# Routing each token to its own expert in the last stage of a two-layer attention kernel

## What is computed

```
x = x + _L1_xattn_ref(ctx, _layernorm(x), ...)      # ends with out @ Wout and a layer norm
x = x + _L1_ffn_ref(_layernorm(x), ...)

logits = xt @ Wg.T                                  # xt: 4096 x 512
top1 = argmax(logits)                               # one expert per token
xhat = layernorm(xt)
for each expert e:
    h = gelu((xhat * s_e + b_e) @ W1_e + b1_e)      # 512 -> 128
    y += (top1 == e) * (h @ W2_e + b2_e)            # 128 -> 512
```

## Time and profile before

| | |
|---|---|
| median of 3 runs | 3383.18 us (3382.89 to 3386.95) |
| profiled execution, its own time | 3382.07 us |
| its span, first to last instruction | 3380.3 us |
| TensorE matmuls busy | 3005.5 us, 89% |
| DVE, ACT, POOL busy | 2083.6, 1558.0, 1327.4 us |
| mean granted TensorE clock | 0.934 of 2.4 GHz |
| DMA | 220.43 MB, mean 65 GB/s |

### The profile page before, as it was taken

How to read it: one execution, slowest core, us unless ns; L and a number is a source line. 1 busy time by engine, 2 the same in 40 slices (tenths; PEclk the granted TensorE clock), 3 DMA queues, 4 the chain that set the end, 5 groups by cost and what they waited for, 6 DMA issues and landing times. The chain is left out here.

```text
span 3380.3 us, 44846 instructions
## 1 busy us (share of the span) xinstructions
PE 3005.5 (89%) x16620; PEld 2534.8 (75%) x16620; DVE 2083.6 (62%) x4123; ACT 1558.0 (46%) x3036; POOL 1327.4 (39%) x913
## 2 busy tenths in 40 slices
PE   6888999968664999999999999999999769999998
PEld 5677777744433898989899898989989657777777
DVE  4766666622365776767777676777767654444432
ACT  2333333311033676767667676766767522222222
POOL 1444444410021465656556565655656530111110
PEclk9899999977765999999999999999999979999999
DMA  5112121112078112121211112111121231111100
GB/s 178 36 46 60 48 61 39 48 66 95 3 267 318 46 34 61 36 61 37 62 37 34 59 37 62 37 59 35 36 62 37 79 127 35 68 50 50 50 25 25
DMA packets 131551, 220.43 MB, mean 65 GB/s; under 512 B 44750, under 2 KB 46799, under 8 KB 127246
## 3 DMA queue, kind: packets, MB, share of 16 engines
q1 hardware_dynamic: 117933, 168.09, 16.4%
q10 hardware_dynamic: 13408, 49.56, 4.0%
HBM read 112.01 MB, written 69.47 MB: 54 GB/s over the span
## 5 line engine op out<-in xcount | busy, mean ns | idle before, releaser
L1635 POOL TENSOR_SCALAR pa_Pr<-pa_Pr,pa_rs 128x590 f32<-128x590 f32 x512 | 904.6, 1771 | 699.9 <-DVE pa_rs L1864 699.9
L1868 DVE TENSOR_REDUCE pa_least<-pa_S 128x1 f32<-128x590 f32 x512 | 391.3, 764 | 242.3 <-PE pa_S L1699 240.4
L1764 ACT ACTIVATE pa_PTh<-pa_W 128x512 fp32r<-128x512 f32 (+1 forms) x640 | 367.7, 596 | 174.4 <-PE pa_W L1710 158.5
L1819 DVE TENSOR_TENSOR pa_PTl<-pa_W,pa_PTh 128x512 fp32r<-128x512 f32 (+1 forms) x640 | 422.0, 683 | 33.2 <-ACT pa_PTh L1764 25.4
L1796 ACT ACTIVATE pa_Pr<-pa_S,pa_least 128x590 f32<-128x590 f32 x512 | 385.2, 752 | 79.3 <-DVE pa_least L1868 76.2
L1710 PE MATMUL pa_W<-pa_ident,pa_Pr 128*128 128x128 f32 (+1 forms) x2560 | 368.7, 275 | 9.7 <-DVE pa_Ql L1834 8.9
L1710 PEld LDWEIGHTS pa_W<-pa_ident,pa_Pr 128*128 128x128 f32 (+1 forms) x2560 | 306.8, 143 | 34.0 <-DVE pa_Ql L1834 12.0
L1724 PE MATMUL pa_O<-pa_PTh,pa_V 128*128 128x512 f32 (+1 forms) x640 | 293.2, 458 | 11.6 <-DVE pa_PTl L1819 8.1
L1697 PE MATMUL pa_S<-pa_U,pa_Qh 128*128 128x296 f32 (+1 forms) x1024 | 234.1, 311 | 44.7 <-DMA pa_Um<-pa_U 44.4
L1725 PE MATMUL pa_O<-pa_PTl,pa_V 128*128 128x512 f32 (+1 forms) x640 | 257.8, 403 | 0.0
L1697 PEld LDWEIGHTS pa_S<-pa_U,pa_Qh 128*128 128x128 f32 x1024 | 180.3, 195 | 71.1 <-DMA pa_Um<-pa_U 47.7
(11 more groups left out here) (400 smaller groups left out, 7223.2 us busy)
## 6 DMA issues: line engine op xcount, KB each, us to landing
pa_Um<-pa_U SPq DMA_DIRECT2D x128, 147.5 KB
pa_Qh<-pa_Qh SPq DMA_DIRECT2D x128, 128.0 KB
o_s<-pa_O_pair SPq DMA_DIRECT2D x64, 256.0 KB, 2.6
ex_o_raw<-o_s SPq DMA_DIRECT2D x8, 2048.0 KB, 10.8
z_s<-la_z_hi ACTq DMA_DIRECT2D x8, 1180.0 KB, 7.6
z_s<-la_z_lo ACTq DMA_DIRECT2D x8, 1180.0 KB, 10.0
pa_z_hi<-z_s ACTq DMA_DIRECT2D x8, 1180.0 KB, 6.0
pa_z_lo<-z_s ACTq DMA_DIRECT2D x8, 1180.0 KB, 10.1
```

The source lines that it names most:

```text
L1635: pool.tensor_scalar(p, p, rs[:, g % 2, t:t + 1], None, ALU.mult).then_inc(*pool_s.mark("probs", n))
L1764: act.activation(out, src, ACT.Copy, scale=scale).then_inc(*act_s.mark("hi", *name))
L1819: dve.tensor_tensor(out, src, f32(hi_ap), ALU.subtract).then_inc(*dve_s.mark(*name))
L1868: dve.tensor_reduce(least[:, g % 2, t:t + 1], scored[n % 2], AX, ALU.min).then_inc(*dve_s.mark("least", n))
```

## The change

Layout. A scratch tensor `xs_s` in DRAM holds 4 regions of 4128 rows of 1028 floats: two experts share a region, one fills it from below and one from above. A row is a token's `xh`, its x, and its number (less 65536) in one column. `wt_s` holds for each expert 128 rows of 2561 floats: W1 high and low, W2 high and low, one column of b1 and a row part of b2.

First half, a round b for each batch (and one more to drain). It does what was done before up to `choice`, one batch behind `read_out`. `ranks` counts for each token how many earlier ones chose the same expert, by a matmul with a triangle of ones and one with running counts kept by POOL. `row_places` makes row numbers of this. POOL's `send(b)` writes the 512 rows of a batch to `xs_s` by four indirect DMAs. W1 and W2 pass through in 8 chunks, one per round, are split and stored to `wt_s`. x, xh and the number share three buffers R, and o has 12 slots in place of 8.

Between the halves, `routes()` computes on DVE from the counts of all experts which 15 tiles of 512 rows there are (15 are enough for any routing), each tile's expert, its rows and its end. Rows past the end and their output are out of bounds and skipped by the DMA.

Second half, 15 tiles i. POOL fetches the 512 rows of a tile (128 partitions by 4 rows) and the 128 rows of its expert's weights by index, and writes out 4 x 128 rows by token number. Weights have two buffers, rows have four.

```diff
+            def send(b):
+                pool.wait_ge(*dve_s.after("place", b))
+                pool.wait_ge(*dve_s.after("xh", b, NT - 1))
+                pool.wait_ge(*pool_s.after("token", b))
                 for t in range(NT):
+                    pool.indirect_dma_start(xs_s, bass.IndirectOffsetOnAxis(ap=place[:, b, t:t + 1], axis=0), R4[b % 3][:, t, :], None)\
+                        .then_inc(free[b % 3], 16)
...
+            def fetch_weights(i):
+                if i >= 2:
+                    pool.wait_ge(*pe_s.after("y", i - 2, NT - 1))
+                n = i % 2
+                pool.indirect_dma_start(f32(Wt[n][:, :]), None, wt_s, bass.IndirectOffsetOnAxis(ap=wsrc[:, i:i + 1], axis=0)).then_inc(wt_in[n], 16)
...
+            for i in range(TILES):
+                pool.wait_ge(*dve_s.after("tok", i))
+                for j in range(NT):
+                    pool.wait_ge(*dve_s.after("free", "y", i, j))
+                    pool.indirect_dma_start(out_rows, bass.IndirectOffsetOnAxis(ap=tok[:, i, j:j + 1], axis=0), R4[buf(i)][:, j, D:2 * D], None,
+                                            bounds_check=TOKENS - 1, oob_is_err=False).then_inc(free[buf(i)], 16)
+                if tile(i + 2):
+                    fetch_weights(i + 2)
+                if tile(i + 3):
+                    fetch_rows(i + 3)
...
+            for b in range(B + 1):
+                if batch(b):
+                    read_out(b, 0)
+                if batch(b - 1):
+                    transposed(b - 1)
+                if batch(b):
+                    read_out(b, 1)
+                if batch(b - 1):
+                    gate_logits(b - 1)
+                if batch(b):
+                    shifts(b)
+                    read_out(b, 2)
+                if batch(b - 1):
+                    gate_rows(b - 1)
+                if batch(b):
+                    read_out(b, 3)
+                if batch(b - 1):
+                    ranks(b - 1)
...
+            for i in range(TILES + 1):
+                first_product(i)
+                for j in range(NT):
+                    second_product(i - 1, j)
+                    row_columns(i + 1, j)
```

In the perceiver, SP fills `xs_s` with zeros, one piece per pair of heads behind `store`:

```diff
+            BLANKS = -(-blanks.shape[0] // PAIRS // 32) * 32
...
+                sp.dma_start(blanks[n0:n1, :].rearrange("(p k) t -> p k t", k=k),
+                             f32(Ql[0][0][P - part:P, :]).unsqueeze(1).to_broadcast([part, k, T])).then_inc(blank, 16)
```

In the slots stage, `S0T` and `WhhT` (in three pieces) are loaded first, and the `gh` products come ahead of the wait for `si`; the copies of `siT` on DVE move behind those of `gh`:

```diff
+            pe.wait_ge(S0_in, 16)
+            for n in range(3):
+                ps = unit("gh", n)
+                pe.wait_ge(Whh_in[n], 16)
...
+            pe.wait_ge(si_in, 16)
             for c in range(C):
                 ps = unit("siT", c)
```

More of the change, by code:

```diff
@@ L1174, in _ @@
                        .then_inc(*dve_s.mark("gh", n, c))
+            for c in range(C):
+                copy(("siT", c), siT[:, c, :])
             dve.wait_ge(*dve_s.at(0, "gh", 2, C - 1))
@@ L1943, in build_experts @@
[L1943 to L1949, removed]
+        Wt = [sb(f"Wt{n}", [P, WW], F32R) for n in range(2)]
@@ L2107, in shut @@
-            def shut(b, e):
-                pe.wait_ge(*dve_s.after("free", "hotT", b))
-                pe.matmul(bank_of["h", b, e][:, :], sel[:, e:e + 1].to_broadcast([P, HE]), hotT[:, :], start=False, stop=True).then_inc(*pe_s.mark("h", b, e))
-            def biases(b):
-                pe.wait_ge(small_cut, 2)
-                pe.wait_ge(*dve_s.after("free", "hotT", b))
-                for t in range(NT):
-                    ps = claim(pe, "out", b, t)
-                    pe.matmul(ps[:, :], hotT[:, t * P:(t + 1) * P], b2[:, :], start=True, stop=False)
@@ L2141, in _ @@
[L2141 to L2172 removed]
+                pe.matmul(ps[:, 0:NT * E], tri[:, :], hot[b % 2][:, :, :].rearrange("p t e -> p (t e)"), start=True, stop=False)
@@ new lines, in ranks, with shifts @@
+                pe.wait_ge(*pool_s.after("cum", b, NT - 1))
+                pe.matmul(ps[:, 0:NT * E], ones[:, :], cum[b % 2][:, :, :].rearrange("p t e -> p (t e)"), start=False, stop=True)\
+                  .then_inc(*pe_s.mark("rank", b))
+            def shifts(n):
+                if n < NCH // 2:
+                    ps = claim(pe, "shift", n)
+                    pe.wait_ge(small, 16 * len(smalls))
+                    pe.wait_ge(raw_in, 16 * (n + 1))
+                    for e in range(EC):
+                        for c in range(C):
+                            k = (n * EC + e) * C + c
+                            m = pe.matmul(ps[:, e:e + 1], raw[:, (e * C + c) * HE:(e * C + c + 1) * HE], shift[:, k:k + 1], start=(c == 0), stop=(c == C - 1))
+                    m.then_inc(*pe_s.mark("shift", n))
@@ new lines, in second_product @@
+            def second_product(i, j):
+                if not tile(i):
+                    return
+                w = Wt[i % 2]
+                ps = claim(pe, "y", i, j)
+                pe.matmul(ps[:, :], bias_rows[:, :], w[:, B2:B2 + D], start=True, stop=False)
+                pe.wait_ge(*dve_s.after("lo", i))
+                product(pe, ps[:, :], [z[:, j * P:(j + 1) * P] for z in h[i % 2]], [w[:, (2 + x) * D:(3 + x) * D] for x in range(2)], False, True)\
+                    .then_inc(*pe_s.mark("y", i, j))
@@ L2174, in _ @@
+            ps = claim(pe, "count")
+            pe.wait_ge(*pool_s.after("cum all"))
+            pe.matmul(ps[:, 0:E], ones[:, :], cum_all[:, :], start=True, stop=True).then_inc(*pe_s.mark("count"))
+            for c in range(C):
+                row_columns(0, c)
+            for i in range(TILES + 1):
+                first_product(i)
+                for j in range(NT):
+                    second_product(i - 1, j)
+                    row_columns(i + 1, j)
         @block.scalar
@@ new lines, in low @@
+            def low(i):
+                dve.wait_ge(*act_s.after("hhi", i))
+                dve.tensor_tensor(h[i % 2][1][:, :], g[i % 2], f32(h[i % 2][0][:, :]), ALU.subtract).then_inc(*dve_s.mark("lo", i))
+            for c in range(C):
+                transposed_lo("rT", 0, c)
+            for i in range(TILES + 1):
+                for j in range(NT):
+                    if tile(i - 1):
+                        result(i - 1, j)
+                    if j == 0 and tile(i):
+                        low(i)
+                    if tile(i + 1):
+                        transposed_lo("rT", i + 1, j)
```

750 lines of the change are left out of this document (440 added, 310 removed).

## The result

| | before | after |
|---|---|---|
| median | 3383.38 us (3382.89 to 3386.95, 4 runs) | 3351.53 us (3351.32 to 3352.04, 4 runs) |
| ratio | | 0.9904, 95% interval 0.9887 to 0.9921 |
| span of the profiled execution | 3380.3 us | 3350.3 us |
| TensorE busy | 3005.5 us, 89% | 2805.0 us, 84% |
| DMA | 220.43 MB | 352.16 MB |

The kernel became 31.9 us faster, 1.0% by the ratio. I had forecast 3385 us, no change: the time lies inside my range, but the side was wrong. One execution, of experiment 5, took 8342 us at a mean granted clock of 0.31; it is left out of that experiment's numbers. Of the 200 us that left TensorE, at most 32 reached the end. These are lines of the page of the kernel after: the busy times, TensorE's clock in 40 slices, and POOL's queue of indirect DMAs.

A forecast was written before the change was run, and what follows sets the result against it. TensorE bounds the last stage before; after, chains through POOL and DMA were to take back its savings. Last stage +14, slots -14, zeros +2 on 3380.3 gave a 3382 us span, forecast 3385 us, range 3300 to 3480.

The forecast's parts named there:

- the landing of a weight fetch: Second half, each tile: 128 rows of 10,244 bytes land in 6.5 us, ends 5.6 and 10.8; enters 13 times.
- (4) to (5): First half, each round: 16 transposes at 0.23 us, from 12.5 to 16.2, then `read_out(b,1)` until 23.0 us.
- (7): First half, round's end: DVE's operations from `outer_norm` to `row_places`, from 31.4 to 44.5 us, 46.5 when folding weights.
- the slots' edit: Slots stage: Whh products start at about 754, ahead of the transposes, so the next products start at 778.7: -14 us.
- zeros: Zero fill of `xs_s`, 67.9 MB, shares the DMA engines with z loads at batch changes: +2 us, ends 0 and 33.
- tail: End of the second half: 17 us from tile 14's first product for its last output and store.
- X: Price of one indirect DMA on POOL: 1.3 us, ends 0.39 and 3.92; enters some 60 times.
- my estimate of 3347: Whole kernel by the Trainium skill's figures, X 1 and landing 5.0 us: 3385 - 18 - 20 = 3347 us.
- (a): Rival: indirect DMAs are cheap, X 0.39 to 0.9 and landing 5.6 us, chains shrink: 3340 us; chance 0.28.
- (b): Rival: TensorE stays the bound, the fetch somehow covered, -259 - 14 us: 3115 us; chance 0.04.
- (c): Rival: TensorE's clock stays at 1.2 GHz throughout the second half's 13 tiles, +60 us: 3445 us; chance 0.18.
- (d): Rival: the zeros delay z and Um loads at each change of batch, +33 us: 3418 us; chance 0.08.

The follow-up runs named there:

- experiment 5: Kernel after with each expert tile's weight fetch issued twice, first into a buffer nobody reads, TensorE waiting for both: 3403.25 us, ratio 1.0054.
- experiment 4: Kernel after with tile i's second products directly following its first product, the next tile's transposes between them, same order on VectorE: 3239.22 us, ratio 0.9575.
- experiment 3: Kernel after with tile 3's inverse deviation moved ahead of the sends and shift additions in POOL's queue: 3322.86 us, ratio 0.9826.
- experiment 1: Kernel after with the slots stage as before, its queries' transposes first and the recurrent product second: 3368.99 us, ratio 0.9960.

## Why the prediction was wrong about the side, and right about the mechanism

I had said that almost none of what leaves TensorE arrives, because both halves hang on chains through POOL and DMA, and 14 of 200 us arrived. What failed is the size of terms in that walk: the landing of a weight fetch, which I put at 6.5 us and which took 5.4 at most; in a round, the steps (4) to (5) and (7), with rounds of 42.5 us on average where I had 44.5 and 46.5; and the slots' edit, worth 18.4 us of span and not 14. Against the walk, in spans, from the windows above:

| step | forecast | measured | difference |
|---|---|---|---|
| slots stage | -14 | -18.4 | -4 |
| zeros (stage begins 17.5 earlier, slots 18.4) | +2 | about +1 | -1 |
| filling and round 1 | 55 + 41 | 98.3 | +2 |
| six rounds | 93 + 178 | 254.8 | -16 |
| between the halves | 71 | 67.0 | -4 |
| twelve tiles | 252 | 238.6 | -13 |
| tail | 17 | 22.1 | +5 |
| span | 3382 | 3350.3 | -31.7 |

**X, 1.3 us: right.** 1.28 from start to start where stores stand back to back, and 5.3 us for the four sends that I put at 5.2. I had only the geometric middle of two plain issues for it (which is 1.24) and the length of another POOL operation, so there was luck in it. I wrote that the forecast hangs on X most of all; it was the term that held.

**The landing of the weights, 6.5 us: the term that failed in the tiles.** I took it from the landings of 1.0 and 1.2 MB on the plain queues. From the issue of the fetch to the first product pass 6.4 us; less the 1.0 of the issue itself that is 5.4 at most, under the lower of my two ends, 5.6. The fetch of tile 14, with no row fetch behind it, takes 6.3 us to its first product, so the row fetch beside the others costs them little. The tile's other parts held: 11.6 us from first product to last sum (11.9), then the store and the fetch. In sum 19.9 instead of 21.0. Experiment 5 shows that this term is on the path, experiment 4 that it need not be. The Trainium skill, "DMA: Bandwidth & Descriptors", section "Anatomy of one DMA", gives 5.0 for it, as an estimate. Its fixed 2.0 us cover the setup of a DMA too, so the 5.0 are to be held against the whole 6.4 us from the start of the issue; by adding an X to them my estimate of 3347 counted part of the setup twice. Here the measurement decides: it is above the page, and the 5.4 are nearest to the 5.6 of the 1024 KB row. With a landing of 5.4 alone, 13 times 1.1 us shorter, the forecast would have been 3371 and the side right. The 1 us that the same page of the Trainium skill gives for the emission by POOL, in section "Latency and other measured facts", agrees with the busy time of the fetch here (0.99); the 0.30 behind it, which the queue pays too, is not in it.

**The rounds, 44.5 and 46.5 us: each 2 to 3 too long.** The first step that failed is (4) to (5): I let all 16 transposes wait for `inner_norm` of tile 3 and start at 12.5 us. Three of them ran before the standstill, and the rest start at 12.2, so `read_out(b,1)` ends at 21.7 instead of 23.0. Step (7), from `outer_norm(b,2)` to the next sends, took 12.3 instead of 13.1. Together these are 2.1 us in this round; I read them in this one alone. The six rounds were 16 us shorter than walked, half of the 31.7. That POOL's queue starts the round was right (4.92 us on TensorE, 7.27 on DVE), and experiment 3 confirms it. But its removal gave 3 us in a round that loads the next o, and not 5 to 7: a second chain, over the landing of the sends and the load of o, lay just beneath.

**The tail, 22.1 us instead of 17, for which I had shown no parts.** From the first product of tile 14 pass 8.0 us to the first store, 9.0 over the eight stores of tiles 13 and 14 on POOL's queue, and 5.2 to the end:

```profile
3328.10 0.76 PE L119 MATMUL ex_bank<-ex_xT_hi,ex_Wt 128*128 128x512 f32 x1 [10.39 <-issue]
```

```profile
3336.12 1.00 POOL L2204 DMA_INDIRECT out<-ex_R,ex_tok  x1 [13.31 <-DVE ex_h_lo L2595]
...
3345.14 0.98 POOL L2204 DMA_INDIRECT out<-ex_R,ex_tok  x1 [0.30 <-issue]
```

**The slots.** Shown by experiment 1: the edit is worth 17.5 us. I had started the products at 754 where Whh's first third was there at 750. So more than half of the measured gain has nothing to do with the experts.

**The rivals.** (a), cheap indirect DMAs at 3340, came nearest in time, but by luck: the landing was short, which is worth 14 us, X was not cheap, and the rest came from the rounds and the slots. Its own terms, 24 to 55 and 12 us off 3385, make 3318 to 3349, so its 3340 was not their middle, 3333. (b) should by its terms be some 3110, not 3115. It did not happen, as argued from the order of instructions; experiment 4 covers the fetch, and even there TensorE is busy 80% of the tiles' time. (c) fell: TensorE starts every tile at 1.2 GHz, as the rule of the Trainium skill, "TensorE: Matmul & The Clock Gate", section "HAM oscillation", has it. The granted clock is 0.50 to 0.64 over the first 4 us of each of the twelve tiles. But it is at 2.4 GHz again about half-way through the burst, as the windows 3129 to 3139 show, and 0.90 or more from 5.6 to 8 us in each tile. My tile had it so. (d) fell: TensorE's idle time on Um in the perceiver grew from 44.4 to 45.7 us.

**The sum.** The forecast of the stage was a difference of two numbers near 700. An error of 1 us in a term that comes six to thirteen times was as large as what I wanted to tell, and five of the seven terms that were off, among them the two that repeat, erred to the same side.

## What to carry to other kernels

When work is made sparse, treat what the busy engine saves as an upper bound and walk the chain that sends out and fetches the rows: here 14 of 200 us arrived. Look at which instruction frees the buffer of the next prefetch: if the consumer stands right behind it, two buffers hide nothing, and a new order of the same instructions is worth more (112 us here) than the sparse stage brought before it (14 us). On a queue that runs in order, put the short operation that others wait for ahead of the long ones that nobody waits for (29 us), and loads that wait for nothing ahead of those that wait (16 us).

## What the runs showed of the hardware

In the tiles an indirect DMA of 128 rows holds POOL for about the same time whether a row has 2 KB (stores, 0.98 us), 10 KB (weights, 0.99) or 16 KB (rows of four tokens, 1.03), with 0.30 us to the next. The sends of the rounds, with rows of 4 KB, took 0.95 to 1.41; no run shows why. A gather of 128 rows of 10 KB is there at most 5.4 us after its issue has ended; a second one ahead of it adds 3.4 us, which for its 1.31 MB is 390 GB/s. In the tiles of experiment 4 the transfers kept the DMA engines at a share of 0.78 and 290 GB/s for 100 us. TensorE's clock came back to 2.4 GHz within 6 us of work after a standstill of 9 us, and with standstills under 4 us (experiment 4) it was granted 0.95 on average.
